# Router logits formed in four column groups of TensorE, and turned back in one step per batch

## The chip, the cores and the metric

The kernel runs on one core of a Trainium2 chip. The metric is the device time of one execution, in microseconds (us). The measured runs give a median over executions; the profile is one further execution, recorded by the hardware profiler.

## What is computed

The input `x` is 8 batches of 512 tokens of 256 values. The reference is two residual blocks:

```python
x = x + attn(cond(x, fside, mask, ...), ...)        # block 1
x = x + ffn(cond2(x, cond_64, ...), ...)            # block 2
```

`cond` is a causal attention with 16 heads of 64 and one shared key and value; `attn` mixes the 16 heads within a token. `cond2` is a mixture of eight experts with two shared ones; its router is the first of the two that the change touches:

```python
logits = (x @ wt.T + repeat(g @ wg.T, s)) / 2       # [4096, 8], x in 256, g in 64 values a batch
scores = softmax(logits); topk_w, topk_idx = top_k(scores, 2)
```

`ffn` is an attention with 16 heads of 16, a layer norm, and a hierarchical mixture of experts with the second router, then a layer norm:

```python
gp = softmax(xt @ w_group + b_group)                # 4 groups
ep = softmax(einsum('td,gde->tge', xt, w_expert) + b_expert)   # 2 experts in each
```

## The kernel before

Everything is float32. The work is cut by batches of 512 tokens (`S`), a batch into four tiles of 128 tokens (`NT`). There are four program parts, each a list of steps in a fixed order. Every engine runs the same list and does its own share of each step, in that order: TensorE (PE) in `tensor_*`, VectorE (DVE) in `vector_*`, ScalarE (ACT) in `scalar_*`, GpSimd (POOL) in `gpsimd_*`, and SyncE (SP), which only starts transfers, in `sync_*`. An engine that waits in a step holds up all of its later steps. `w.wait_ge(at(name, key))` waits for the step that signals `did(name, key)`; waits that are already known to be met are left out. Between parts all engines meet (`meet`, L2640).

**Part one** is `cond` for all batches and `attn` for all but the last.

**Part two** (`order_tail`, then `order_two`) begins with the steps `e_weights` and `x_last`. In `e_weights` SP loads the first router's weights (`wt`, `wg`, `cT`, `before`), then seven batches of the first block's result from memory (`e_x`, 512 KB each), the shared experts' weights and some tables. In `x_last` it loads the last batch's input, four tiles, to which POOL adds a bias (L988). The parts of the last batch's `attn` (`hs`, `hv`: products on POOL and DVE at L829, sums on DVE at L841) are woven with the first router's steps and with the shared experts (`shared`, L1246, L1257). The first router's steps are

- `r_init`, one step behind the first part of the woven list `one`: PE forms `g @ wg.T` for the batches (L1201), ACT halves it into `cs` (L1523), DVE fills `ones` (L1310);
- `r_turn`: PE turns a batch's tiles (L1208), ACT writes them to `e_xT` (L1528);
- `r_score`: PE multiplies with `wt`, 8 weight columns against 512 tokens, in two halves of the contraction (L1215); ACT adds `cs` and writes `e_lgT`, 8 partitions by 512 (L1533);
- `r_back`: four transposes turn 8x128 pieces into 128x8 ones in one bank (L1227);
- `r_lgc`, `r_soft`, `r_rank`, `r_cnt`, `r_oh`, `count`, for lots of 3, 4 and 1 batches: softmax, the two best experts and each token's place in its expert's list (mostly DVE). Then POOL scatters the tokens (L1578), and after `slots` it fetches them by expert.

Batches 0 to 6 pass turn, score and back early in part two; the last one at its end, since it needs the last `attn`.

**Part three** is the attention of `ffn`, with the second router at its end. The attention computes scores in four row groups of the array (L1842, L1863), exponentials on ACT (`m_pt`, L2022), and the products with the values in four column groups (`m_av`, L1877):

```python
for j in range(4):
    i = pe.matmul(m.ap[32 * j:32 * j + 32, :], v.ap[:, kt, 4 * g + j, :], p.ap[:, j, :],
                  start=(kt == 0), stop=(kt == NT - 1), tile_position=(0, 32 * j))
```

In the last slot but one of batch 6 (`h_tables`) SP loads the second router's weights and tables, and DVE fills `h_ones` (L2248). Early in batch 7 (`h_load`, L2140) SP loads six batches back (`h_x`), once every store of them is done. In batch 7 the steps `h_turn` (L2177, L2459), `h_score` (L2184, L2464) and `h_back` (L2196) of batches 0 to 5 stand in the slots between the attention's own steps, one triple to three slots; those of batches 6 and 7 follow behind the attention (`last_rows`, L1681 on). They are like the first router's with 12 logits in place of 8. `h_gate` and `h_count`, for lots of 6, 1 and 1 batches, choose the expert (DVE); then POOL scatters (L2489).

**Part four** fetches the tokens by expert, runs the experts, the last layer norm, and writes the output.

Of the kernel before, what the change touches and what calls it, by code (L numbers as in the profile page):

```python
# [175 lines left out]
def at(name, *key):  # L176
    return (name, *key)
# [32 lines left out]
def cols(t):  # L210
    return t[tuple(slice(None) for _ in t.shape)]
# [847 lines left out]
def setup_two(k, nc, ins):  # L1059
# [6 lines left out]
    k.wt = sb("ew_wt", [P, 2, E8])  # L1066
    k.wg = sb("ew_wg", [DH, E8])
# [42 lines left out]
    k.lgT = Ring([sb(f"e_lgT{i}", [E8, S]) for i in range(2)])  # L1110
    k.cs = sb("e_cs", [E8, NB])
# [11 lines left out]
    k.end2 = at_.pos  # L1123

# [5 lines left out]
def route_ring(k, b):  # L1130

    return k.rR if b < NB - 1 else k.rM


def sync_two(k, sp, w, order):
    did, ins = k.c.did, k.ins

    def load(name, i, dst, src):
        sp.dma_start(dst, src).then_inc(*did("d_" + name, i))

    for step, *key in order:
# [53 lines left out]
def tensor_two(k, pe, w, order):  # L1195
    did, ident = k.c.did, k.ident
    for step, *key in order:
        if step == "r_init":
            m = k.rR.take(("cs",), at("e_csc", 0))
            w.wait_ge(at("d_router", 3), m.room)  # L1200
            pe.matmul(m.ap[0:E8, 0:NB], k.wg[:, :], k.cT[:, :], start=True, stop=True).then_inc(*did("e_cs", 0))  # L1201
# [104 lines left out]
def vector_two(k, dv, w, order):  # L1306
    did = k.c.did
    for step, *key in order:
        if step == "r_init":
            dv.memset(k.ones[:, :], 1.0).then_inc(*did("e_ones", 0))  # L1310
        elif step == "r_lgc":
# [3 lines left out]
            dv.tensor_copy(k.lg[:, n0:n1, :], k.rL.of(g).ap[:, 0:(n1 - n0) * E8].rearrange("p (t e) -> p t e", e=E8)).then_inc(*did("e_lgc", g))  # L1315
# [161 lines left out]
def route(k, dv, w, step, g):  # L1477
# [26 lines left out]
    elif step == "r_cnt":  # L1504
        prior = k.before[:, :, :].unsqueeze(1).broadcast_to([P, GT, E8, E8])
        w.wait_ge(at("r_k", g, 0), at("d_router", 3))
        dv.tensor_tensor(c1, c1, prior, ALU.mult).then_inc(*did("r_c", g, 0))
        w.wait_ge(at("r_c", g, 0), at("r_k", g, 1))
        dv.tensor_tensor(c0, c0, c1, ALU.add).then_inc(*did("r_c", g, 1))
        w.wait_ge(at("r_c", g, 1))  # L1510
        dv.tensor_reduce(gv, c0, AX, ALU.add).then_inc(*did("r_c", g, 2))
    else:
        w.wait_ge(at("r_c", g, 2))
        dv.tensor_scalar(k.oh[:, n0:n1, 0, :], gv, 0.5, None, ALU.is_lt)
        dv.tensor_scalar(k.oh[:, n0:n1, 1, :], gv, 1.0, None, ALU.is_equal).then_inc(*did("r_oh2", g))


def scalar_two(k, ac, w, order):
    did = k.c.did
    for step, *key in order:  # L1520
        if step == "r_init":
            w.wait_ge(at("e_cs", 0))
            ac.activation(k.cs[:, :], k.rR.of(("cs",)).ap[0:E8, 0:NB], ACT.Copy, scale=0.5).then_inc(*did("e_csc", 0))  # L1523
# [5 lines left out]
        elif step == "r_score":  # L1529
# [3 lines left out]
            ac.activation(l.ap[:, :], route_ring(k, b).of(("score", b)).ap[0:E8, :], ACT.Identity, bias=k.cs[:, b:b + 1], scale=0.5).then_inc(*did("e_lgT", b))  # L1533
# [557 lines left out]
def setup_four(k, nc, ins):  # L2093
# [4 lines left out]
    k.hlgT = Ring([e["mx"](f"h_lgT{i}", [12, S]) for i in range(2)])  # L2098
# [12 lines left out]
    k.wgx = e["end"]("hw_gx", [P, 2, 12])  # L2111
    k.bgx = e["end"]("hw_bgx", [12, 1])
# [23 lines left out]
def sync_four(k, sp, w, order):  # L2136
    did, ins = k.c.did, k.ins

    def load(name, i, dst, src):
        sp.dma_start(dst, src).then_inc(*did("d_" + name, i))  # L2140

    for step, *key in order:
        if step == "h_tables":
            load("gx", 0, k.wgx[:, :, 0:4], ins["w_group"].rearrange("(c p) g -> p c g", p=P))
            load("bg", 0, k.bgx[0:4, :], ins["b_group"].rearrange("(n o) -> n o", o=1))
            load("bx", 0, k.bgx[4:12, :], ins["b_expert"].rearrange("(n o) -> n o", o=1))
# [302 lines left out]
def scalar_four(k, ac, w, order):  # L2449
    did, ins = k.c.did, k.ins  # L2450

    for step, *key in order:
# [7 lines left out]
        elif step == "h_score":  # L2460
# [3 lines left out]
            ac.activation(l.ap[:, :], k.hA.of(("score", b)).ap[0:12, :], ACT.Identity, bias=k.bgx[:, 0:1]).then_inc(*did("h_lgT", b))  # L2464
# [271 lines left out]
```

## Time and profile before

| | us |
|---|---|
| median of 3 runs | 2408.55 |
| lowest and highest run | 2406.16, 2410.59 |
| span of the profiled execution | 2401.5 |
| PE busy | 2053.0 (85%) |
| DVE busy | 1528.3 (64%) |
| ACT busy | 1161.6 (48%) |
| POOL busy | 1068.8 (45%) |

For the profiled execution its span is the only time given, from its first instruction to its last; the median of the runs is 7.05 us above it. Part two runs from about 1098 to its last expert; the second router's steps run from 2071 to 2209.

How to read the rows: times are in us from the span's start unless marked ns. PE is a matmul, PEld a weight load of TensorE; SPq is the queue in which SP starts transfers. `out<-in` are the program's names with buffer numbers left out; `128*32 128x512` is a weight tile of 128 rows and 32 columns and a moving tile of 128 partitions and 512 elements. One float32 matmul of the program appears as two instructions, a transpose as one. `[11.66 <-POOL prod L829]` is idle time before an instruction, and what ended it.

### The profile page before, as it was taken

Reading aid. Unit: us, or ns where it says so; the run is one execution under the profiler, and the core shown is the slowest. Engines: PE = TensorE matmul, PEld = TensorE weight load, DVE = VectorE, ACT = ScalarE, POOL = GpSimd, SP = SyncE. Lnnn points to the kernel's source line nnn. Section 1 sums busy time; section 2 is a strip of 40 time slices with the busy share of each in tenths; the row PEclk is TensorE's granted clock in tenths of the full one; section 3 lists DMA queues with packets and bytes.
Section 4 is the critical chain, followed back from the end, with each engine's and each line's share of the span. In section 5 each row is a group of like instructions: output and inputs, shape, how many; then the busy total and the mean of one; then the engine's idle time right before and its main releaser. Section 6 shows DMA issues by size and latency. Waiting matters only on the chain.

```text
span 2401.5 us, 33727 instructions
## 1 busy us (share of the span) xinstructions
PE 2053.0 (85%) x11536; PEld 1111.7 (46%) x11536; DVE 1528.3 (64%) x3276; ACT 1161.6 (48%) x2718; POOL 1068.8 (45%) x840
## 2 busy tenths in 40 slices
PE   2999899999989998985678976889999998873997
PEld 1555555555555555552345863223333332221664
DVE  1345868686776768685964545667667766434776
ACT  0776666666666666662112341345555454541221
POOL 0104747474756658474576532112222201117686
PEclk9999999999999999997889997899999999996998
DMA  7315352434410000005035643111111150203232
GB/s 250 116 36 170 101 194 88 132 108 139 136 34 13 14 7 5 14 5 152 25 112 166 194 155 90 43 35 40 45 53 50 40 193 18 73 10 106 78 92 75
DMA packets 175729, 204.60 MB, mean 85 GB/s; under 512 B 19305, under 2 KB 157417, under 8 KB 175306
## 3 DMA queue, kind: packets, MB, share of 16 engines
q1 hardware_dynamic: 116826, 112.57, 14.8%
q0 software_dynamic: 16752, 45.84, 6.3%
q10 hardware_dynamic: 41984, 44.04, 5.4%
q8 instruction: 95, 1.56, 0.3%
q14 instruction: 72, 0.59, 0.1%
HBM read 83.75 MB, written 114.46 MB: 83 GB/s over the span
## 4 chain that ended last, share of the span: by engine, by line
PE 59%; DVE 14%; POOL 9%; ACT 9%; issue 5%; DMA 2%; ACTq 2%; SPq 1%; POOLq 0%; DVEq 0%
PE ps L1863 11%; POOL prod L829 8%; ACT m_pt L2022 6%; PE ps L561 4%; PE ps L588 4%; PE ps L547 3%; PE ps L572 3%; PE ps L598 3%; DVE sc L841 3%; PE ps L1877 3%; DVE pb L712 3%; PE ps L2224 3%; PE ps L1285 3%; PE ps L2232 2%; PE ps L1821 2%
## 5 line engine op out<-in xcount | busy, mean ns | idle before, releaser
L1954 DVE TENSOR_REDUCE m_mx<-ps 128x2 f32<-128x1024 f32 x256 | 311.6, 1224 | 172.3 <-PE ps L1842 171.6
L712 DVE CUSTOM_DVE_ANT_0 pb<-ps,bias,snl 128x128 f32<-128x128 f32 (+3 forms) x512 | 260.4, 547 | 226.6 <-PE ps L561 223.7
L2022 ACT ACTIVATE m_pt<-ps 128x1024 f32<-128x1024 f32 x256 | 260.5, 1024 | 289.2 <-PE ps L1863 289.2
L829 POOL TENSOR_TENSOR prod<-qs,kvs 128x1024 f32<-128x1024 f32 x120 | 283.7, 2390 | 171.8 <-issue 133.0
L829 POOL TENSOR_TENSOR prod<-sc,kvs 128x1024 f32<-128x1024 f32 x120 | 280.5, 2369 | 101.9 <-ACT sc L947 85.8
L1863 PE MATMUL ps<-m_q,m_k 32*128 32x512 f32 x1024 | 274.2, 647 | 50.8 <-ACT m_pt L2022 39.9
L907 ACT ACTIVATE pb<-pb,mst 128x129 f32<-128x129 f32 (+3 forms) x512 | 283.4, 560 | 16.9 <-DVE mst L712 14.9
L1842 PE MATMUL ps<-m_k,m_q 32*128 32x512 f32 x1024 | 276.3, 660 | 8.9 <-DVE m_mx L1954 8.3
L561 PE MATMUL ps<-kz,qT 64*128 64x128 f32 (+3 forms) x1024 | 185.5, 441 | 0.0
L2041 POOL DMA_INDIRECT m_yg<-ye_scratch,e_pos x64 | 63.1, 986 | 270.4 <-DVE m_x L1942 233.1
L572 PE MATMUL ps<-ident,pb 128*128 128x128 f32 x1280 | 179.8, 279 | 0.5 <-DVE mst L712 0.4
L841 DVE TENSOR_REDUCE sc<-prod 128x64 f32<-128x1024 f32 x128 | 152.3, 1210 | 43.1 <-POOL prod L829 42.8
L922 ACT ACTIVATE ptb<-ps 128x384 f32<-128x384 f32 (+1 forms) x256 | 135.5, 545 | 68.9 <-PE ps L572 68.4
L588 PE MATMUL ps<-ptb,vt 128*64 128x512 f32 (+3 forms) x1024 | 156.9, 449 | 11.6 <-DVE xr L786 11.6
L572 PEld LDWEIGHTS ps<-ident,pb 128*128 128x128 f32 x1280 | 140.9, 141 | 55.9 <-issue 43.5
L841 DVE TENSOR_REDUCE ob<-prod 128x64 f32<-128x1024 f32 x128 | 153.2, 1211 | 9.8 <-POOL prod L829 9.8
L1863 PEld LDWEIGHTS ps<-m_q,m_k 32*128 32x128 f32 x1024 | 73.2, 185 | 174.2 <-ACT m_pt L2022 150.4
L1877 PE MATMUL ps<-m_pt,m_va 128*32 128x512 f32 x1024 | 140.5, 612 | 0.0
L547 PE MATMUL ps<-xnT,w_wq 128*128 128x512 f32 x256 | 122.1, 599 | 13.1 <-DVE oTT L724 13.1
L598 PE MATMUL ps<-w_wo,oTT 128*128 128x256 f32 x512 | 122.3, 382 | 3.0 <-DVE oTT L724 3.0
L2054 POOL TENSOR_TENSOR m_lnrs<-m_lnve,mhalf 128x1 f32<-128x1 f32 x32 | 18.1, 565 | 227.9 <-DVE m_lnve L797 227.9
L588 PEld LDWEIGHTS ps<-ptb,vt 128*64 128x64 f32 x1024 | 70.8, 140 | 94.1 <-issue 83.5
(329 smaller groups left out, 3837.4 us busy)
## 6 DMA issues: line engine op xcount, KB each, us to landing
xh_scratch<-zt SPq DMA_DIRECT2D x43, 768.0 KB, 8.2
xe_scratch<-zt ACTq DMA_DIRECT2D x32, 1024.0 KB, 4.5
ye_scratch<-e_ys SPq DMA_DIRECT2D x36, 256.0 KB, 2.1
hw_w<-in_w SPq DMA_DIRECT2D x16, 512.0 KB, 6.0
xin<-in_x SPq DMA_DIRECT2D x8, 512.0 KB, 3.6
bias<-in_fside ACTq DMA_DIRECT2D x8, 512.0 KB, 10.6
y_scratch<-e_y SPq DMA_DIRECT2D x8, 512.0 KB, 3.2
m_x<-y_scratch SPq DMA_DIRECT2D x8, 512.0 KB, 4.1
```

Source lines behind the costliest of these rows:

```text
L561: pe.matmul(ms[j].ap[:, 0:n], q.ap[DH * j:DH * j + DH, t * P:(t + 1) * P], kz.ap[DH * j:DH * j + DH, 0:n], start=False, stop=True, tile_po ...
L572: i = pe.transpose(m.ap[:, j * P:(j + 1) * P], pb[:, SEG[t] + kt * P:SEG[t] + (kt + 1) * P], ident[:, :])
L588: i = pe.matmul(m.ap[DH * j:DH * j + DH, kt * P:S], v.ap[:, kt, :], turned(pt.ap, kt), start=(kt == 0), stop=(kt == NT - 1), tile_position ...
L712: dv.tensor_tensor_reduce(pb.ap[:, j, SEG[t]:SEG[t] + n], rS.of(("S", b, p, t, j)).ap[:, 0:n], k.bias[:, h, CAUSAL[t]:CAUSAL[t + 1]], -1.0 ...
L829: e.tensor_tensor(out, one, two, ALU.mult).then_inc(*k.c.did(*product_done(step, b, t, u)))
L841: dv.tensor_reduce(heads(dst.ap[:, :])[:, 4 * u:4 * u + 4, :], src, AX, ALU.add).then_inc(*k.c.did(step + "_r", b, t, u))
L907: ac.activation(part, part, ACT.Exp, bias=ms[:, 0, j, t:t + 1], scale=-1.0, accum_out=ms[:, 1, j, t:t + 1]).then_inc(*did("exp", b, p, t, j))
L1842: x = pe.matmul(m.ap[:, i, :], band(q.ap, j)[:, t * P:(t + 1) * P], band(kk.ap, j), start=True, stop=True, tile_position=(32 * j, 0))
L1863: x = pe.matmul(m.ap[:, i, :], band(kk.ap, j)[:, kt * P:(kt + 1) * P], band(q.ap, j), start=True, stop=True, tile_position=(32 * j, 0))
L1877: i = pe.matmul(m.ap[32 * j:32 * j + 32, :], v.ap[:, kt, 4 * g + j, :], p.ap[:, j, :], start=(kt == 0), stop=(kt == NT - 1), tile_position ...
L1954: dv.tensor_reduce(x.ap[:, t, 64 * half:64 * half + 64].rearrange("p (i r) -> p i r", i=2)[:, :, 16], score_ring(k, b).of((b, g, t, half)) ...
L2022: ac.activation(p.ap[:, 2 * half:2 * half + 2, :], k.qE.of((b, g, kt, half)).ap, ACT.Exp).then_inc(*did("m_exp", b, g, kt, half))
```

## The change

Both routers: the weights are padded to 32 columns, and each of a batch's four tiles gets its own column group of the array, so that the logits of tile `t` lie in partitions `32t` and on, over 128 tokens. The eviction is 128x128 in place of 8x512 or 12x512. One transpose (first router), or one matmul with columns picked from the identity (second), turns a whole batch's logits back. The padding is filled with zeros by DVE, and SP waits for that before it loads the weights. The biases are loaded once for each group.

```diff
+BAND = 32
@@ setup_two
-    k.wt = sb("ew_wt", [P, 2, E8])
-    k.wg = sb("ew_wg", [DH, E8])
+    k.wt = sb("ew_wt", [P, 2, BAND])
+    k.wg = sb("ew_wg", [DH, NT, BAND])
-    k.lgT = Ring([sb(f"e_lgT{i}", [E8, S]) for i in range(2)])
-    k.cs = sb("e_cs", [E8, NB])
+    k.lgT = Ring([sb(f"e_lgT{i}", [P, P]) for i in range(2)])
+    k.cs = sb("e_cs", [P, NB])
+def bands(ap, rows):
+    return ap.rearrange("p (t r) -> p t r", r=BAND)[:, :, 0:rows]
@@ sync_two, e_weights
-            load("router", 0, cols(k.wt), ...)
-            load("router", 1, cols(k.wg), ins["moe_wg"])
-            load("router", 2, cols(k.cT), ins["condT"][:, 0:NB])
-            load("router", 3, cols(k.before), ins["c_before"])
+            w.wait_ge(at("e_pad", 0), at("e_pad", 1))
+            load("router", 0, k.wt[:, :, 0:E8], ...)
+            for t in range(NT):
+                load("router", 1 + t, k.wg[:, t, 0:E8], ins["moe_wg"])
+            load("router", NT + 1, cols(k.cT), ins["condT"][:, 0:NB])
+            load("router", NT + 2, cols(k.before), ins["c_before"])
@@ tensor_two
-            pe.matmul(m.ap[0:E8, 0:NB], k.wg[:, :], k.cT[:, :], start=True, stop=True).then_inc(*did("e_cs", 0))
+            pe.matmul(m.ap[:, 0:NB], k.wg[:, :, :].rearrange("p t r -> p (t r)"), k.cT[:, :], start=True, stop=True)...
             for c in range(2):
-                i = pe.matmul(m.ap[0:E8, :], k.wt[:, c, :], k.exT[:, b, c, :], start=(c == 0), stop=(c == 1))
+                for t in range(NT):
+                    i = pe.matmul(band(m.ap, t)[:, 0:P], k.wt[:, c, :], k.exT[:, b, c, t * P:(t + 1) * P],
+                                  start=(c == 0), stop=(c == 1), tile_position=(0, BAND * t))
@@ r_back
-            for t in range(NT):
-                n = b * NT + t - LOT[g][0]
-                i = pe.transpose(m.ap[:, n * E8:(n + 1) * E8], l.ap[:, t * P:(t + 1) * P], ident[0:E8, 0:E8])
-            i.then_inc(*did("e_lgb", b))
+            n = b - LOT[g][0] // NT
+            pe.transpose(m.ap[:, n * P:(n + 1) * P], l.ap[:, :], ident[:, :]).then_inc(*did("e_lgb", b))
@@ vector_two, r_init
+            dv.memset(k.wt[:, :, :], 0.0).then_inc(*did("e_pad", 0))
+            dv.memset(k.wg[:, :, :], 0.0).then_inc(*did("e_pad", 1))
             dv.memset(k.ones[:, :], 1.0).then_inc(*did("e_ones", 0))
@@ scalar_two, r_score
-            ac.activation(l.ap[:, :], route_ring(k, b).of(("score", b)).ap[0:E8, :], ACT.Identity, ...)
+            ac.activation(l.ap[:, :], route_ring(k, b).of(("score", b)).ap[:, 0:P], ACT.Identity, ...)
@@ setup_four
-    k.hlgT = Ring([e["mx"](f"h_lgT{i}", [12, S]) for i in range(2)])
+    k.hlgT = Ring([e["mx"](f"h_lgT{i}", [P, P]) for i in range(2)])
-    k.wgx = e["end"]("hw_gx", [P, 2, 12])
-    k.bgx = e["end"]("hw_bgx", [12, 1])
+    k.wgx = e["end"]("hw_gx", [P, 2, BAND])
+    k.bgx = e["end"]("hw_bgx", [P, 1])
@@ sync_four, h_tables
+            w.wait_ge(at("h_pad", 0), at("h_pad", 1))
             load("gx", 0, k.wgx[:, :, 0:4], ...)
-            load("bg", 0, k.bgx[0:4, :], ins["b_group"]...)
-            load("bx", 0, k.bgx[4:12, :], ins["b_expert"]...)
+            for t in range(NT):
+                load("bg", t, k.bgx[BAND * t:BAND * t + 4, :], ins["b_group"]...)
+                load("bx", t, k.bgx[BAND * t + 4:BAND * t + 12, :], ins["b_expert"]...)
@@ tensor_four
             for c in range(2):
-                i = pe.matmul(m.ap[0:12, :], k.wgx[:, c, :], xt.ap[c][:, :], start=(c == 0), stop=(c == 1))
+                for t in range(NT):
+                    i = pe.matmul(band(m.ap, t)[:, 0:P], k.wgx[:, c, :], xt.ap[c][:, t * P:(t + 1) * P],
+                                  start=(c == 0), stop=(c == 1), tile_position=(0, BAND * t))
@@ h_back
-            for t in range(NT):
-                n = b * NT + t - HLOT[g][0]
-                i = pe.transpose(m.ap[:, n * 12:(n + 1) * 12], l.ap[:, t * P:(t + 1) * P], ident[0:12, 0:12])
-            i.then_inc(*did("h_lgb", b))
+            n = 12 * (b * NT - HLOT[g][0])
+            pe.matmul(m.ap[:, n:n + 12 * NT], l.ap[:, :], bands(ident[:, :], 12), start=True, stop=True)...
@@ vector_four, h_tables
+            dv.memset(k.wgx[:, :, :], 0.0).then_inc(*did("h_pad", 0))
+            dv.memset(k.bgx[:, :], 0.0).then_inc(*did("h_pad", 1))
             dv.memset(k.hones[:, :], 1.0).then_inc(*did("h_ones", 0))
```

DVE's copies of the logits (L1315, L2405) and the waits for the loads follow the new places and counts.

## Rows read from the trace of the kernel before

**Rows 1.** Timeline of SP's queue, from 1098: start, us, line, transfer, count.

```profile
1098.89 0.38 SPq L1139 DMA_DIRECT2D ew_wt<-in_moe_wt  x1
1099.32 0.48 SPq L1139 DMA_DIRECT2D ew_wg<-in_moe_wg  x1
...
1113.41 1.85 SPq L490 DMA_DIRECT2D e_x<-in_x  x4
```

**Rows 2.** Timeline of POOL, same stretch; idle before, and releaser, in brackets.

```profile
1119.88 2.77 POOL L988 TENSOR_TENSOR e_x<-e_x,w_bout 128x256 f32<-128x256 f32 x4 [22.11 <-DMA e_x<-in_x]
```

**Rows 3.** Chain of waits in part two: start, us, engine, output, line.

```profile
1114.83 4.92 DMA e_x<-in_x
...
1144.50 2.57 PE ps L1215 x4
...
1269.39 1.90 PE ps L1215 x4
```

**Rows 4.** Timeline of DVE in part two.

```profile
1110.94 0.17 DVE L1310 MEMSET e_ones<- 128x128 f32 x1
...
1124.97 1.22 DVE L841 TENSOR_REDUCE sc<-prod 128x64 f32<-128x1024 f32 x1 [11.66 <-POOL prod L829]
...
1142.14 0.42 DVE L753 TENSOR_TENSOR qs<-ps,w_bq 128x256 f32<-128x256 f32 x1 [2.52 <-PE ps L635]
...
1150.21 0.25 DVE L1492 TENSOR_REDUCE e_sm<-e_lg 128x12 f32<-128x96 f32 x1 [2.37 <-ACT e_lg L1538]
```

**Rows 5.** Chain of waits at the end of part three, scores of batches 2, 6, 7.

```profile
2108.63 1.82 PE ps L2184 x4
...
2163.85 3.14 PE ps L2184 x4
...
2189.07 3.60 PE ps L2184 x4
```

**Rows 6.** Timeline of POOL at the end of part three.

```profile
2178.89 0.73 POOL L2054 TENSOR_TENSOR m_lnrs<-m_lnve,mhalf 128x1 f32<-128x1 f32 x1 [1.47 <-DVE m_lnve L797]
...
2201.25 0.97 POOL L2489 DMA_INDIRECT xh_scratch<-h_x,h_sposi  x1 [0.30 <-issue]
2204.80 1.05 POOL L2489 DMA_INDIRECT xh_scratch<-h_x,h_sposi  x1 [2.58 <-issue]
```

**Rows 7.** L1877: its first four matmuls; all eight, with loads; durations ns min/median/max.

```profile
2122.90 0.64 PE L1877 MATMUL ps<-m_pt,m_va 128*32 128x512 f32 x4
...
2122.90 0.16 PEld L1877 LDWEIGHTS ps<-m_pt,m_va 128*32 128x32 f32 x8 [0.17 <-issue]
2122.90 1.06 PE L1877 MATMUL ps<-m_pt,m_va 128*32 128x512 f32 x8
...
L1877 PEld LDWEIGHTS ps<-m_pt,m_va x1024: 106/109/156, 1532.8 to 2157.5; 128*32 128x32 f32 x171
```

**Rows 8.** ACT: the line L1533 (ns min/median/max), and L941 among the groups (us, ns).

```profile
L1533 ACT ACTIVATE e_lgT<-ps,e_cs x8: 662/678/679, 1113.1 to 1271.3; 8x512 f32<-8x512 f32 x8
...
L941 ACT ACTIVATE kvs<-ps 128x256 f32<-128x256 f32 x32 | 12.2, 380 | 27.8 <-PE ps L641 27.8
```

**Rows 9.** Timeline of PE, a batch's `r_back`.

```profile
1118.68 0.41 PE L1227 MATMUL ps<-ident,e_lgT 8*128 8x8 f32 x4 [0.77 <-ACT e_lgT L1533]
```

**Rows 10.** Timelines of SP, DVE and PE around `h_tables` and `h_load`.

```profile
2071.84 0.44 SPq L2140 DMA_DIRECT2D hw_gx<-in_w_group  x1
...
2072.87 0.17 DVE L2248 MEMSET h_ones<- 128x128 f32 x1
...
2080.92 4.67 SPq L2140 DMA_DIRECT2D h_x<-x_scratch  x6
...
2085.31 0.66 PE L2177 MATMUL ps<-ident,h_x 128*128 128x128 f32 x4 [0.43 <-DMA h_x<-x_scratch]
...
2087.40 0.66 PE L2177 MATMUL ps<-ident,h_x 128*128 128x128 f32 x4 [1.43 <-ACT h_xT L2459]
```

**Rows 11.** One stretch: length, busy by engine (instructions), granted clock, DMA share, GB/s.

```profile
2104.50:2113.00 8.50, 7.92 (x41) 2.73 (x42) 0.00 (x0) 3.64 (x7) 0.00 (x0) 0.80 0.00 0
```

More of the change, by code:

```diff
@@ L1142, in sync_two @@
         if step == "e_weights":
-            load("router", 0, cols(k.wt), ins["moe_wt"].rearrange("(c p) e -> p c e", p=P))
-            load("router", 1, cols(k.wg), ins["moe_wg"])
-            load("router", 2, cols(k.cT), ins["condT"][:, 0:NB])
-            load("router", 3, cols(k.before), ins["c_before"])
+            w.wait_ge(at("e_pad", 0), at("e_pad", 1))
+            load("router", 0, k.wt[:, :, 0:E8], ins["moe_wt"].rearrange("(c p) e -> p c e", p=P))
+            for t in range(NT):
+                load("router", 1 + t, k.wg[:, t, 0:E8], ins["moe_wg"])
+            load("router", NT + 1, cols(k.cT), ins["condT"][:, 0:NB])
+            load("router", NT + 2, cols(k.before), ins["c_before"])
             for b in range(NB - 1):
@@ L1199, in tensor_two @@
             m = k.rR.take(("cs",), at("e_csc", 0))
-            w.wait_ge(at("d_router", 3), m.room)
-            pe.matmul(m.ap[0:E8, 0:NB], k.wg[:, :], k.cT[:, :], start=True, stop=True).then_inc(*did("e_cs", 0))
+            w.wait_ge(at("d_router", NT + 2), m.room)
+            pe.matmul(m.ap[:, 0:NB], k.wg[:, :, :].rearrange("p t r -> p (t r)"), k.cT[:, :], start=True, stop=True).then_inc(*did("e_cs", 0))
         elif step == "r_turn":
@@ L1314, in vector_two @@
             n0, n1 = LOT[g]
-            dv.tensor_copy(k.lg[:, n0:n1, :], k.rL.of(g).ap[:, 0:(n1 - n0) * E8].rearrange("p (t e) -> p t e", e=E8)).then_inc(*did("e_lgc", g))
+            dv.tensor_copy(k.lg[:, n0:n1, :], bands(k.rL.of(g).ap[:, 0:(n1 - n0) * BAND], E8)).then_inc(*did("e_lgc", g))
         elif step in ("r_soft", "r_rank", "r_cnt", "r_oh"):
@@ L1505, in route @@
         prior = k.before[:, :, :].unsqueeze(1).broadcast_to([P, GT, E8, E8])
-        w.wait_ge(at("r_k", g, 0), at("d_router", 3))
+        w.wait_ge(at("r_k", g, 0), at("d_router", NT + 2))
         dv.tensor_tensor(c1, c1, prior, ALU.mult).then_inc(*did("r_c", g, 0))
@@ L1522, in scalar_two @@
             w.wait_ge(at("e_cs", 0))
-            ac.activation(k.cs[:, :], k.rR.of(("cs",)).ap[0:E8, 0:NB], ACT.Copy, scale=0.5).then_inc(*did("e_csc", 0))
+            ac.activation(k.cs[:, :], k.rR.of(("cs",)).ap[:, 0:NB], ACT.Copy, scale=0.5).then_inc(*did("e_csc", 0))
         elif step == "r_turn":
@@ L1532, in scalar_two @@
             w.wait_ge(at("e_lg", b), at("e_csc", 0), l.room)
-            ac.activation(l.ap[:, :], route_ring(k, b).of(("score", b)).ap[0:E8, :], ACT.Identity, bias=k.cs[:, b:b + 1], scale=0.5).then_inc(*did("e_lgT", b))
+            ac.activation(l.ap[:, :], route_ring(k, b).of(("score", b)).ap[:, 0:P], ACT.Identity, bias=k.cs[:, b:b + 1], scale=0.5).then_inc(*did("e_lgT", b))
         elif step == "r_soft":
@@ L2143, in sync_four @@
         if step == "h_tables":
+            w.wait_ge(at("h_pad", 0), at("h_pad", 1))
             load("gx", 0, k.wgx[:, :, 0:4], ins["w_group"].rearrange("(c p) g -> p c g", p=P))
-            load("bg", 0, k.bgx[0:4, :], ins["b_group"].rearrange("(n o) -> n o", o=1))
-            load("bx", 0, k.bgx[4:12, :], ins["b_expert"].rearrange("(n o) -> n o", o=1))
+            for t in range(NT):
+                load("bg", t, k.bgx[BAND * t:BAND * t + 4, :], ins["b_group"].rearrange("(n o) -> n o", o=1))
+                load("bx", t, k.bgx[BAND * t + 4:BAND * t + 12, :], ins["b_expert"].rearrange("(n o) -> n o", o=1))
             for g in range(4):
@@ L2193, in tensor_four @@
             w.wait_ge(at("h_lgT", b))
-            for t in range(NT):
-                n = b * NT + t - HLOT[g][0]
-                i = pe.transpose(m.ap[:, n * 12:(n + 1) * 12], l.ap[:, t * P:(t + 1) * P], ident[0:12, 0:12])
-            i.then_inc(*did("h_lgb", b))
+            n = 12 * (b * NT - HLOT[g][0])
+            pe.matmul(m.ap[:, n:n + 12 * NT], l.ap[:, :], bands(ident[:, :], 12), start=True, stop=True).then_inc(*did("h_lgb", b))
         elif step == "h_count":
@@ L2463, in scalar_four @@
             w.wait_ge(at("h_lg", b), at("m_mT", NB - 1, G4 - 1), l.room)
-            ac.activation(l.ap[:, :], k.hA.of(("score", b)).ap[0:12, :], ACT.Identity, bias=k.bgx[:, 0:1]).then_inc(*did("h_lgT", b))
+            ac.activation(l.ap[:, :], k.hA.of(("score", b)).ap[:, 0:P], ACT.Identity, bias=k.bgx[:, 0:1]).then_inc(*did("h_lgT", b))
         elif step == "h_gate":
```

4 lines of the change are left out of this document (2 added, 2 removed).

## The prediction

> **What bounds the kernel now.** I read the profile's page, the chain of waits, the queue of the sync engine (SP), and then each step that the change touches, in order of time. TensorE (PE) is busy for 85% of the span, but the change is decided where engines wait, so I work by place and not by share.
>
> *First place, the start of the second program part.* SP issues `e_weights` and behind it the four loads of `x_last` [rows 1]. GpSimd (POOL) waits 22.11 us for those loads before its `e_x` [rows 2]. The chain of waits runs through just this: SP's issues, the DMA `e_x<-in_x`, `e_x`, `prod`, VectorE's (DVE) `sc` [rows 3]; DVE stands idle 11.66 us in front of that `sc` [rows 4]. So a microsecond that SP loses ahead of `x_last` is lost by all.
>
> *Second place, the end of the third part.* In the last attention batch PE and ScalarE (ACT) take turns, and the second router's scores stand on the chain [rows 5]. Behind it the logits of batches 6 and 7 are links of a serial chain, with POOL's scatters beside it [rows 5, 6].
>
> **A score.** Before, 4 matmuls of 512 columns take 1.90 us at full clock [rows 3]: 4 rounds of 0.43 and a tail of 0.17. After there are 16 of 128 columns. Do column groups overlap? The attention's `L1877` has that form, 32 weight columns at four positions: its eight 512-column matmuls take 1.06 us, the first four together 0.64, their eight weight loads 0.16 [rows 7]; in single file eight would take 3.6. So I take 4 rounds of 0.107 (a quarter of 0.43) and the tail, 0.6 us, and allow 0.1 for 32 instructions where there were 8: 0.7 us, gain 1.2. At half clock 3.60 [rows 5] becomes 4 x 0.213 + 0.2 = 1.05. Bounds: 0.6 us, and the old 1.90 if nothing overlaps.
>
> **The eviction.** ACT's 8x512 takes 0.68 us [rows 8]. No row shows 128x128 from such a source; 128x256 takes 0.38 [rows 8] and is an upper bound but for the bias. I take 0.35, gain 0.33 (bounds 0.2 and 0.4).
>
> **The turn back.** Four small transposes take 0.41 us [rows 9]; one full transpose I take as 0.27, gain 0.13 (a loss is excluded: it is one of the four with more columns). In the second router it becomes a matmul, two weight loads and two short passes for four of each: I take no gain, and up to 0.2 lost where it can no longer run beside `L1863`, whose rows of the array it now uses too.
>
> **Term 1, SP's new wait.** `e_weights` now waits for `e_pad`, which DVE writes in `r_init`. DVE comes there at 1110.94, where it fills `e_ones` now, in 0.17 [rows 4]; two more such fills, overlapping, end at 1111.2. SP begins at 1111.3 in place of 1098.89 [rows 1]: 12.4 us. Then `ew_wg` is loaded four times, three more at 0.48 and a gap [rows 1]: 1.5. Queued behind: the seven `e_x` loads, the shared experts' weights, the tables, `x_last`, and then the experts' weights, which nobody needs before they are in. The whole train moves: **+13.9 us** (low end 12.4, the extra loads free). PE's `r_init` waits too, some 8 us, and its first turn for `e_x`, but the scores of batches 0 to 2, about 3.5 us each then, are through before ACT's late `sc`, behind which they are held now as well.
>
> **Term 2, inside the first router.** The chain passes `e_lgT`, `L1227`, `L635`, then `L1215` at half clock, 2.57 us [rows 3], and `e_lgT` again; DVE idles 2.52 and 2.37 us for it [rows 4]. Of the first idle 0.6 goes (eviction and turn), of the second 1.9 (a score 1.5 shorter, an eviction 0.33), of which PE may give back 0.8 by being at half clock for the next turns. **-2.1** (ends -1.5, -2.5). The other batches' scores lie beside DVE's work: nothing.
>
> **Term 3, its last batch.** Turn, score [rows 3], eviction, back, copy in a row with nothing beside them: 1.2 + 0.33 + 0.13, **-1.65**.
>
> **Term 4, SP in the third part.** `h_tables` waits for two more fills on DVE, where `h_ones` is filled at 2072.87: SP starts at 2073.15 in place of 2071.84, 1.3 us [rows 10]. Six more tiny loads, each somewhat under the 0.44 of the first one [rows 10], 2.3 us. `h_load` is the next step but one on this queue, with no gap, and PE's first `h_turn` already waits for its first landing [rows 10]: 3.6 us later. Its second turn waits 1.43 us for ACT, until 2087.40 [rows 10]; of that I estimate 0.75 as ACT still finishing `m_pt`, which will be over by then. **+2.85** (end 3.6; no delay at all is excluded by the DMA as the releaser in that row).
>
> **Term 5, batches 0 to 5 of the second router.** In even ones `L2184` [rows 5] stands before `L1863`, for which ACT waits: 1.6 (partly half clock) + 1.2 + 1.2. In odd ones the eviction is queued behind two `m_pt` of ACT, and once the score is short ACT is what is late: I take 0.75, 0.25 and 1.0. Together 6.0, less 0.5 for PE being longer at half clock after Term 4's stall: **-5.5** (ends -3.5, -7.5).
>
> **Term 6, batches 6 and 7.** Scores of 3.14 and 3.60 at half clock [rows 5] lose 2.0 and 2.6, an eviction 0.33: 4.9 us on DVE's chain. But POOL's scatters run back to back until 2202.2, with little but one wait of 1.47 us in them [rows 6]. They would end at about 2200.5, and the last batch's would start 0.3 behind them, at 2200.8 in place of 2204.80 [rows 6]: **-4.0** (end -3.3).
>
> **Sum:** 13.9 - 2.1 - 1.65 + 2.85 - 5.5 - 4.0 = **+3.5 us**. The profiled span of 2401.5 becomes 2405.0; what lies between it and the median, 7.05, I leave: 2408.55 becomes **2412.0 us**. A measurement of this kernel can tell about 0.2% (4.8 us) from no change, so this is the upper half of no change. With the low ends, and with the high ends, the case reaches from 2407 to 2416.5.
>
> **Rivals.**
> - *The weight loads are not hidden.* Each round then pays a load of 0.109 [rows 7] and 0.107 of columns: 4 x 0.216 + 0.17 = 1.03 us, 0.33 more than forecast at full and some 0.65 at half clock, 3.2 over the scores that count: +6.7, 2415.2 us, slower. Against: the loads of `L1877`'s second round lie within its first [rows 7]. For: that round lasts 0.43, a new one 0.107, no longer than a load. 10%. The Trainium skill (TensorE: Matmul & The Clock Gate, Part 3) states that a weight load overlaps matmuls in flight only if it goes to another row group, which these never do. By that rule this rival is the case; `L1877`'s eight loads in 0.16 us speak against the rule.
> - *The column groups don't overlap at 128 columns.* 16 x 0.107 + 0.17 = 1.88: the score gains nothing, Terms 2, 3, 5 and 6 shrink to -0.9, -0.5, -0.5, -0.5: +14.4, 2423 us, slower. It decides from a score of some 1.4 us on. Against: rows 7. 7%.
> - *PE's clock.* PE has less to do in the last attention batch, and the granted clock is down to 0.80 in one stretch there already [rows 11]. If two more stretches of 9 us fell from full to that, 1.8 us each: +7.1, 2415.7 us, slower. 8%.
> - *The wait doesn't count.* If `x_last` were covered, Term 1 is gone: -10.4, 2398 us, faster. Against: 22.11 us of idle time in front of it [rows 2]. For: DVE has idle stretches behind it, where some could be caught up. 9%.
>
> **How the numbers follow.** 66% for the forecast's case: 46 within 0.2%, 17 above, 3 below. With the rivals: slower 17 + 10 + 7 + 8 = 42%, same 46%, faster 3 + 9 = 12%. The range, 2404 to 2421, leaves out the last rival and the second, and a few hundredths at the case's own edges.
>
> **What would show it.** SP's `ew_wt` at about 1111.3; POOL's `e_x` at 1133.8; a score of 16 matmuls in 0.7 us, an eviction of 0.35; `h_tables` issued behind DVE's fills, and PE waiting some 3 us more for the first `h_x`; the last batch's scatters 0.3 us behind the others. The prediction is wrong if POOL's `e_x` isn't some 13 us late, if a stage behind it takes that up, or if a score takes over 1 us.

## The result, and the profile of the kernel after

The changed kernel takes 2410.15 us (median of 12 runs, 2406.49 to 2416.83), the kernel before, on the same chip, 2404.43 us (12 runs, 2398.50 to 2410.59). The ratio is 1.0028, with a 95% interval of 1.0015 to 1.0041: slower by 6.7 us (3.6 to 9.9; the medians alone differ by 5.7), a little more than the 0.2% that can be told from no change. The profiled execution spans 2405.5 us where that of before spanned 2401.5, so the profiles can explain only 4.0 us of the difference. The twelve executions of the kernel after have mean granted clocks of TensorE between 0.946 and 0.952; the profile of before has 0.955.

First SP's queue and its followers in part two, from the timeline of the kernel after (start, duration, engine, instruction, idle time before it and what ended it), which answer to [rows 1, 2, 4]:

```profile
1109.07 0.11 DVE L1318 MEMSET ew_wt<- 128x64 f32 x1
1109.39 0.38 SPq L1145 DMA_DIRECT2D ew_wt<-in_moe_wt  x1
...
1114.93 0.59 PE L1209 MATMUL ps<-ew_cT,ew_wg 64*128 64x8 f32 x2 [7.57 <-DMA ew_before<-in_c_before]
...
1124.91 1.86 SPq L491 DMA_DIRECT2D e_x<-in_x  x4
1130.43 2.76 POOL L989 TENSOR_TENSOR e_x<-e_x,w_bout 128x256 f32<-128x256 f32 x4 [34.73 <-DMA e_x<-in_x]
1135.51 1.22 DVE L842 TENSOR_REDUCE sc<-prod 128x64 f32<-128x1024 f32 x1 [23.86 <-POOL prod L830]
```

SP starts right behind DVE's fills. POOL's `e_x` begins 10.55 us later than before and DVE idles 23.86 us in front of `sc`, where it idled 11.66 us before. This execution's first part had run 1.87 us ahead of the other's (DVE's fill is at 1109.07, not at 1110.94), though nothing in the first part was changed; so the delay that the change makes here is 10.55 + 1.87 = 12.4 us.

The last batch of the first router, in the chain of waits after (start, duration, what), answers to the last scores of [rows 3]:

```profile
1277.58 0.69 PE ps L1224 x16
1278.27 0.02 issue
1278.30 0.38 ACT e_lgT L1543
1278.67 0.14 issue
1278.81 0.31 PE ps L1236
1279.12 0.02 issue
1279.14 0.20 DVE e_lg L1325
```

A score of 0.69 us in place of 1.90, an eviction of 0.38 in place of 0.69, a turn of 0.31 in place of 0.40. Then the shared expert (`L1254` after, `L1246` before), in windows of PE (length, PE busy, granted clock, DMA share, GB/s), after and then before:

```profile
1295.00:1300.00 5.00, 5.00 (x10) 0.71 0.26 105
```

```profile
1291.00:1296.00 5.00, 5.00 (x16) 1.00 0.15 52
```

The third part, SP and PE in the timeline of after, against [rows 10]:

```profile
2081.55 0.38 SPq L2150 DMA_DIRECT2D hw_gx<-in_w_group  x1
...
2091.93 4.28 SPq L2150 DMA_DIRECT2D h_x<-x_scratch  x6
...
2096.30 0.82 PE L2189 MATMUL ps<-ident,h_x 128*128 128x128 f32 x4 [2.80 <-DMA h_x<-x_scratch]
2097.89 1.11 PE L2189 MATMUL ps<-ident,h_x 128*128 128x128 f32 x4 [0.77 <-ACT h_xT L2473]
2100.64 1.08 PE L2197 MATMUL ps<-h_xT,hw_gx 128*32 128x128 f32 x16
```

And its end, POOL's scatters and the conversion of their indices on DVE, against [rows 6]:

```profile
2201.66 0.17 DVE L2354 CAST h_sposi<-h_spos 128x4 int32<-128x4 f32 x1
...
2204.04 1.17 POOL L2503 DMA_INDIRECT xh_scratch<-h_x,h_sposi  x1 [0.30 <-issue]
2207.76 0.96 POOL L2503 DMA_INDIRECT xh_scratch<-h_x,h_sposi  x1 [2.54 <-issue]
```

POOL is free at 2205.2 and the indices are there since 2201.8, yet the last batch's first scatter starts at 2207.76. It was 2204.80 before, where the indices came at 2202.5, just behind POOL's coming free at 2202.2:

```profile
2202.31 0.17 DVE L2340 CAST h_sposi<-h_spos 128x4 int32<-128x4 f32 x1
```

The fourth part begins 3.1 us later than before (2220.66 less 2217.55), but its first transposes of `h_hb` are 4.2 later. PE's timeline after, then before:

```profile
2220.66 1.08 PE L2227 MATMUL ps<-ident,h_xs 128*128 128x128 f32 x4 [21.19 <-DMA h_xs<-xh_scratch,h_gix]
2221.93 3.78 PE L2236 MATMUL ps<-hw_w,h_sT 128*128 x4 [0.19 <-ACT h_sT L2489]
...
2227.86 0.60 PE L2252 MATMUL ps<-ident,h_hb 128*128 128x128 f32 x4
```

```profile
2217.55 1.09 PE L2215 MATMUL ps<-ident,h_xs 128*128 128x128 f32 x4 [17.50 <-DMA h_xs<-xh_scratch,h_gix]
2218.83 3.08 PE L2224 MATMUL ps<-hw_w,h_sT 128*128 x4 [0.19 <-ACT h_sT L2475]
...
2223.69 0.60 PE L2240 MATMUL ps<-ident,h_hb 128*128 128x128 f32 x4
```

The same instructions take longer after PE's idle time: their five us from 2221.8 on run at a granted clock of 0.54, the corresponding five of before, from 2218.7 on, at 0.76.

### The profile page after: what moved, and what is told of

It reads as the page before. It is cut to its first block, busy times and chain, and to the rows that moved or that the text cites. A ratio compares the mean times of both kernels' runs of the same rounds, so it can differ in the third digit from the quotient of the medians.

```text
span 2405.5 us, 34045 instructions
## 1 busy us (share of the span) xinstructions
PE 2039.3 (85%) x11688; PEld 1118.0 (46%) x11688; DVE 1528.2 (64%) x3280; ACT 1156.3 (48%) x2718; POOL 1068.5 (44%) x840
## 4 chain that ended last, share of the span: by engine, by line
PE 57%; DVE 13%; POOL 10%; ACT 9%; issue 5%; DMA 2%; ACTq 2%; SPq 1%; POOLq 0%; DVEq 0%
PE ps L1873 11%; POOL prod L830 8%; ACT m_pt L2032 6%; PE ps L589 4%; PE ps L562 4%; PE ps L548 3%; PE ps L573 3%; PE ps L599 3%; DVE sc L842 3%; DVE pb L713 3%; PE ps L1887 3%; PE ps L1293 3%; PE ps L1831 2%; PE ps L2236 2%; PE ps L2244 2%
```

## The experiments

Each ratio is to the kernel before on the same chip in the same session. That matters for the first four, which ran on a chip where the kernel before took 2443 us; on the others it took 2401 to 2403. "Under the kernel after" means under its ratio of 1.0028, which was measured in another session; such differences are uncertain by some 4 to 6 us.

**1. The wait alone, in the kernel before.**

```diff
+            dv.memset(k.wt[:, :, :], 0.0).then_inc(*did("e_pad", 0))
+            dv.memset(k.wg[:, :], 0.0).then_inc(*did("e_pad", 1))
             dv.memset(k.ones[:, :], 1.0).then_inc(*did("e_ones", 0))
...
+            w.wait_ge(at("e_pad", 0), at("e_pad", 1))
             load("router", 0, cols(k.wt), ins["moe_wt"]...)
```

> The kernel before, whose DVE fills ew_wt and ew_wg (in their old small shapes) in r_init, and whose SP waits for these fills ahead of e_weights; nothing else of the change. Term 1 alone (the wait is on the path, with nothing behind it to take it up): ew_wt issued at about 1109 to 1111 in place of 1098.9, POOL's e_x later by the same 10.5 to 12.4 us, and the whole 10 to 12.4 us slower (ratio about 1.0045). The wait doesn't count (rival): POOL's e_x is as late, but the time is within 2 us of before. The wait costs because of the loads' number and not of the wait: no delay at all at POOL's e_x.

Ratio 1.0049 (1.0033 to 1.0066), 12 us slower. From its timeline:

```profile
1108.79 0.38 SPq L1139 DMA_DIRECT2D ew_wt<-in_moe_wt  x1
1128.95 2.78 POOL L988 TENSOR_TENSOR e_x<-e_x,w_bout 128x256 f32<-128x256 f32 x4 [33.25 <-DMA e_x<-in_x]
```

One wait for two fills of 0.07 us costs more than the whole change does. Some of the 12 us may be clock, since these executions also have the lower mean granted clock (0.943 to 0.953, the kernel before 0.946 to 0.955). The rival that the wait doesn't count falls.

**2. The change with its two fills earlier.** DVE has 7.6 us of idle time at the head of part two; the fills move there, SP's wait stays.

```diff
-        if step == "r_init":
+        if step == "e_weights":
             dv.memset(k.wt[:, :, :], 0.0).then_inc(*did("e_pad", 0))
             dv.memset(k.wg[:, :, :], 0.0).then_inc(*did("e_pad", 1))
+        elif step == "r_init":
             dv.memset(k.ones[:, :], 1.0).then_inc(*did("e_ones", 0))
```

> The kernel after, with DVE's two fills moved from r_init to the head of its part two, where its idle time of 7.6 us lies; SP's wait stays. Term 1 is the wait: SP issues ew_wt at about 1099, POOL's e_x comes 10 to 12 us earlier than in after, and the time is 10 to 12 us under after, about 5 under before (ratio to before about 0.998). If the three more loads of ew_wg were what costs, or if the wait didn't count: within 2 us of after (ratio to before 1.002 to 1.003).

0.9980 (0.9965 to 0.9995): 4.9 us faster than before, so some 11.7 under the kernel after (1.0028 less 0.9980, of 2443). From its timeline:

```profile
1096.75 0.11 DVE L1318 MEMSET ew_wt<- 128x64 f32 x1 [0.18 <-DVEq L2655]
1097.09 0.38 SPq L1145 DMA_DIRECT2D ew_wt<-in_moe_wt  x1
...
1119.27 2.76 POOL L989 TENSOR_TENSOR e_x<-e_x,w_bout 128x256 f32<-128x256 f32 x4 [23.74 <-DMA e_x<-in_x]
```

The three more loads of `ew_wg` are still there, and they are not free: `e_x` follows `ew_wt` by 22.18 us here and by 21.04 in the kernel after, where run 1, without them, has 20.16. That is 1 to 2 us, small against the wait.

**3 and 4. `x_last` ahead of `e_weights` on SP's queue,** once in the kernel after, once in the kernel before.

```diff
-    out = [("e_weights",), ("x_last",)] + [x for part in start for x in part]
+    out = [("x_last",), ("e_weights",)] + [x for part in start for x in part]
```

> The kernel after, with SP's x_last ahead of e_weights and its wait. Reading of term 1 by x_last alone (PE's own lateness behind the router's weights costs nothing): POOL's e_x no longer waits, DVE's 23.9 us of idle time in front of sc shrink to a few, 12 us or more under after. Rival, term 1 has two roads: the router's weights and the e_x loads come late as well, PE's r_init and its first turn (now 7.6 and 1.8 us idle) hold the first part's last batch in PE's queue, and only a part comes back, 0 to 8 us under after.

> The kernel before with SP's x_last ahead of e_weights, nothing of the change. If the x_last load is what the stage waits for, DVE's 11.7 us of idle time in front of sc go but for what the late router weights (1.8 us later) give back: 7 to 11 us under before (ratio 0.9955 to 0.997). If it is covered by something else that is nearly as late: within 3 us of before.

In the kernel after: 0.9942 (0.9920 to 0.9964), 21 us under it. In the kernel before: 0.9954 (0.9936 to 0.9972), 11 us under it. POOL and PE in the timeline of the first, then POOL in that of the second:

```profile
1100.94 2.77 POOL L989 TENSOR_TENSOR e_x<-e_x,w_bout 128x256 f32<-128x256 f32 x4 [5.63 <-DMA e_x<-in_x]
1115.93 0.59 PE L1209 MATMUL ps<-ew_cT,ew_wg 64*128 64x8 f32 x2 [8.84 <-DMA ew_before<-in_c_before]
```

```profile
1099.67 2.77 POOL L988 TENSOR_TENSOR e_x<-e_x,w_bout 128x256 f32<-128x256 f32 x4 [5.80 <-DMA e_x<-in_x]
```

DVE has no idle time left in front of `sc` in either. The 11 us of before are the 11.66 of [rows 4]; the kernel after gets these and a good part of the wait. But not all of it: PE still idles 8.84 us for the router's weights. What that costs shows in the time from PE's start in part two (`L622`, 1096.89 in the kernel after, 1098.96 before) to POOL's first scatter (1181.09, 1172.16): 73.2 us before, 84.2 after, 73.2 in run 2, 61.5 in run 4, 66.4 in run 3, and 60.5 in run 12 below, which has run 2's fills as well (60.7 in run 7, which has them too). So with `x_last` first the wait still costs 5.9 us (66.4 less 60.5) by way of PE. Both theories of the expectation were half right: the second road, by way of PE, is real, but it was the shorter one, and the gain was far above the 8 us that this theory allowed.

**5. The four matmuls of a column group in a row.** In both scores.

```diff
-            for c in range(2):
-                for t in range(NT):
+            for t in range(NT):
+                for c in range(2):
                     i = pe.matmul(band(m.ap, t)[:, 0:P], ...)
```

> The kernel after; in both scores the loop over the four column groups is outside and that over the two halves of the sum inside, so that four matmuls in a row go to one group and only the ends of the groups can run side by side: 13 rounds in place of 4. If the short score comes of the groups running side by side, the 16 matmuls take 13 x 0.107 + 0.17 = 1.6 us at full clock (0.65 in after), 2.9 at half, and the time rises by 7 to 12 us over after (ratio to before about 1.006). If it comes of the 128 columns alone or of cheaper instructions, the score stays at 0.65 and the time is that of after (1.003).

1.0029 (1.0016 to 1.0042), the kernel after over again. PE and ACT in its timeline:

```profile
1278.00 0.67 PE L1224 MATMUL ps<-e_xT,ew_wt 128*32 128x128 f32 x16 [0.79 <-ACT e_xT L1538]
1278.76 0.37 ACT L1543 ACTIVATE e_lgT<-ps,e_cs 128x128 f32<-128x128 f32 x1 [0.81 <-PE ps L1224]
```

ACT starts 0.76 us after the score does, 0.72 in the kernel after (1278.30 less 1277.58), so it isn't a matter of how ends are recorded. My expectation of 1.6 us failed. Either the groups had nothing to do with it, or PE doesn't need them in turn.

**10. Groups apart (made to decide that).** Unused matmuls in PE's idle time in `r_init`.

```diff
+            for i in range(8):
+                pe.matmul(band(m.ap, i % NT)[:, 0:P], ident[:, 0:BAND], ident[:, :], start=True, stop=True, tile_position=(0, BAND * (i % NT)))
+            for i in range(8):
+                pe.matmul(band(m.ap, 0)[:, 0:P], ident[:, 0:BAND], ident[:, :], start=True, stop=True, tile_position=(0, 0))
+            for i in range(8):
+                pe.matmul(m.ap[0:E8, 0:P], ident[:, 0:E8], ident[:, :], start=True, stop=True)
+            for i in range(2):
+                pe.matmul(m.ap[0:E8, :], ident[:, 0:E8], ident[:, :].unsqueeze(1).broadcast_to([P, NT, P]), start=True, stop=True)
```

> The kernel after with 26 more matmuls (52 instructions) on PE in r_init, where it is idle for 7.6 us; their output is not used. Eight of 128 columns in turn over the four column groups; eight of 128 columns all in the first group; eight of 128 columns with 8 weight columns and no group named; two of 512 columns with 8 weight columns. At full clock 128 columns have been worth 0.107 an instruction. If groups run side by side: 16 instructions take 16 x 0.107 / 4 = 0.43 in turn over the groups and 1.7 all in one group. If each narrow matmul is simply quick: 0.43 to 0.6 for both. The form without a group: 1.7 if columns count, 0.43 to 0.6 if narrow weights alone make it quick. The last: 1.7 (4 x 0.43). Time as after's.

PE's timeline, matmuls and then weight loads (PEld):

```profile
1109.48 0.64 PE L1210 MATMUL ps<-ident 128*32 128x128 f32 x16
1109.95 1.91 PE L1212 MATMUL ps<-ident 128*32 128x128 f32 x16
1111.69 1.91 PE L1214 MATMUL ps<-ident 128*8 128x128 f32 x16
1113.44 1.88 PE L1216 MATMUL ps<-ident 128*8 128x512 f32 x4
...
1109.48 0.38 PEld L1210 LDWEIGHTS ps<-ident 128*32 128x32 f32 x16 [0.76 <-issue]
1109.84 1.75 PEld L1212 LDWEIGHTS ps<-ident 128*32 128x32 f32 x16
```

The one execution took 2410.2 us. From start to start: 0.47 us in turn over four groups, 1.74 all in one, 1.75 without a group. The factor is 3.7. The groups do run side by side, and narrow weights alone bring nothing. Together with run 5: four groups are needed, but not in turn. How far ahead in its queue PE takes a matmul for a free group was not measured.

**6. `h_tables` ten steps earlier.**

```diff
-        out[30].append(("h_tables",))
+        out[20].append(("h_tables",))
```

> The kernel after, with the step h_tables (the second router's fills and 22 loads) ten steps earlier in part three, on all engines. If term 4 is what SP's queue costs (measured +1.9 us at PE's second turn), SP's h_x loads come earlier, PE's 2.8 us of idle time in front of its first h_turn go, and the time is 1.5 to 3 us under after (ratio to before 1.0015 to 1.002), with an earlier point only if the table loads were on the path before the change too. If h_x's own waits bind, h_x is no earlier and nothing changes.

1.0054 (1.0036 to 1.0071): slower than the kernel after by 6 us. PE's wait for the first `h_x` is gone, but a worse one has come. Its chain of waits, then POOL in its timeline:

```profile
2072.88 0.44 SPq L2150
2073.32 0.04 issue
2073.37 2.16 DMA m_z<-y_scratch
```

```profile
2075.59 0.72 POOL L2059 TENSOR_TENSOR m_z<-m_z,mw_bo 128x256 f32<-128x256 f32 x1 [11.31 <-DMA m_z<-y_scratch]
```

Ten us of table loads now stand in front of `m_z`, which DVE and then PE (idle 4.94 us) need. I had looked at who stands behind the tables at step 30 and not at step 20.

**7. All three moves** (2, 3 and 6 together).

> The kernel after with all three moves: DVE's fills of ew_wt and ew_wg at the head of part two, SP's x_last ahead of e_weights, h_tables ten steps earlier. The x_last move alone gave 0.9942 of before, with PE still idle 8.8 and 1.8 us behind the late router weights. If those waits were on the path: another 4 to 9 us there and 2 from the tables, 0.990 to 0.992. If DVE is the bound there once x_last is early: 2 to 3 us in all, 0.993.

0.9927 (0.9915 to 0.9940): 17.5 us faster than before, with run 6's loss in it. That is the figure I gave for DVE as the bound, but run 6's loss, which I hadn't counted, is in it, and the stretch to the first scatter shortened from 66.4 to 60.7 us; so the late router weights had been on the path, and the ratio alone doesn't decide.

**8. Marks on POOL** ahead of the late scatter.

```diff
+            if n == HLOT[HLAST][0]:
+                po.memset(k.hnil[:, 0:4], 0.0)
+                w.wait_ge(at("h_gs", n // NT))
+                po.memset(k.hnil[:, 4:8], 0.0)
+                w.wait_ge(at("h_id", n // NT))
+                po.memset(k.hnil[:, 8:12], 0.0)
             w.wait_ge(at("h_gs", n // NT), at("h_id", n // NT), at("hc_pos", hlot(n // NT)))
+            if n == HLOT[HLAST][0]:
+                po.memset(k.hnil[:, 12:16], 0.0)
```

> The kernel after with four memsets of 128x4 on POOL as marks ahead of the last batch's first h_scatter: before its waits, after the wait for h_gs, after that for h_id, after that for hc_pos. In after POOL was free at 2205.2, all three were fulfilled by 2201.8, and the scatter started at 2207.8. If a late signal holds POOL, the 2.5 us lie between the marks. If the gap is POOL's own (its next code or its descriptors), they lie before the first mark or behind the last one, and the marks themselves cost about 0.1 us each; if it is a cost of waiting at all, each mark has a share. Time within 2 us of after.

1.0035 (1.0016 to 1.0053). POOL's timeline, the first and the last mark and the scatter:

```profile
2206.03 0.12 POOL L2504 MEMSET h_nil<- 128x4 f32 x1
...
2206.14 0.12 POOL L2511 MEMSET h_nil<- 128x4 f32 x1
2208.39 0.96 POOL L2512 DMA_INDIRECT xh_scratch<-h_x,h_sposi  x1 [2.13 <-issue]
```

All waits are passed by 2206.14; the 2.13 us lie behind the last mark, in the DMA itself. No signal is late. A count shows more: in each of the twelve profiles with this kernel's 4096 bytes for descriptors, the scatters stop behind their 28th, in part two (2.27 us at 1239.75 before) as in part three. (In the four profiles of the slower chip the stop in part three is 6.2 to 8.3 us, which the next expectation overlooks.)

**9. A larger store for POOL's descriptors.** Two small tiles of the first part lie elsewhere to make room.

```diff
-    nc = bacc.Bacc("TRN2", target_bir_lowering=False, num_devices=1, dynamic_dma_scratch_size=4096)
+    nc = bacc.Bacc("TRN2", target_bir_lowering=False, num_devices=1, dynamic_dma_scratch_size=4608)
```

> The kernel after with 4608 bytes in place of 4096 for the descriptors of POOL's DMAs (two small tiles of the first part lie elsewhere for that). In every trace so far a run of scatters stands still for 2.1 to 2.6 us behind its 28th, wherever its data are (29th and 57th of part two, 29th of part three). Theory: the store of descriptors is full after 28 and POOL waits until the last is through; with an eighth more that comes after 32. Then the 29th scatter of part two follows in 0.3 us and the 33rd does not, the 29th scatter of part three follows in 0.3 us, the last four lie about 2.2 us earlier, and the time is 2 to 4.5 us under after (ratio to before about 1.0015). Rival, it is POOL's code that has to be fetched or something else of the place: the gaps stay behind the 28th, time that of after.

1.0026 (1.0011 to 1.0041), no gain. But the stop has moved, by three scatters and not by four. The 31st and the 32nd scatter of part three in its timeline, and the first fetch behind them:

```profile
2210.55 0.96 POOL L2503 DMA_INDIRECT xh_scratch<-h_x,h_sposi  x1 [0.30 <-issue]
2213.90 0.96 POOL L2503 DMA_INDIRECT xh_scratch<-h_x,h_sposi  x1 [2.39 <-issue]
2217.42 0.97 POOL L2511 DMA_INDIRECT h_xs<-xh_scratch,h_gix  x1 [2.56 <-SPq L2654]
```

Part two's stops moved alike, from the 29th and 57th DMA to the 32nd and 63rd: a period of 28 became one of 31 with an eighth more room. So the store's size sets it. There are 32 scatters, so the stop still fell inside them and was still paid. One more place would have put it behind them; no memory was left for that, and it wasn't tried.

**11. The third part's queue shortened.** Fills ten steps earlier, the six more loads behind the first `h_x`, tables in place.

```diff
-        if step == "h_tables":
+        if step == "h_fill":
             dv.memset(k.wgx[:, :, :], 0.0).then_inc(*did("h_pad", 0))
             dv.memset(k.bgx[:, :], 0.0).then_inc(*did("h_pad", 1))
+        elif step == "h_tables":
             dv.memset(k.hones[:, :], 1.0).then_inc(*did("h_ones", 0))
...
+        out[20].append(("h_fill",))
         out[30].append(("h_tables",))
```

> The kernel after; DVE's fills of hw_gx and hw_bgx come ten steps earlier, so that SP's wait ends at once, and the six more loads of hw_bgx stand behind the first load of h_x in place of ahead of it; the tables stay where they are. Term 4 (a later queue of SP makes PE's first h_turn late, +1.9 measured): SP's first load of h_x is issued 3 us earlier, PE's 2.8 us of idle time there go to about 0.4, and the time is 1 to 2.5 us under after (ratio to before about 1.002). If PE loses it again in batch 0 behind ACT: within 1 us of after.

1.0023 (1.0012 to 1.0034). The 0.0005 under the kernel after is 1.2 us and less than the intervals; the profiles show it more sharply: PE's first `h_turn` has no wait,

```profile
2092.29 0.66 PE L2193 MATMUL ps<-ident,h_x 128*128 128x128 f32 x4
2094.87 0.66 PE L2193 MATMUL ps<-ident,h_x 128*128 128x128 f32 x4 [1.93 <-ACT h_xT L2478]
```

and the last batch's first scatter is at 2204.72 where it was 2207.76, of which 0.8 us were there in part two already. So the wait is shown to be SP's queue, but a gain in the time isn't shown.

**12. The best of all:** 2, 3, 9 and 11 together.

> The kernel after with all that the runs so far favour: DVE's fills of the first router at the head of part two, x_last first on SP's queue, the second router's fills early and its six loads behind the first h_x, and 4608 bytes for POOL's descriptors. The first two with the tables moved (which cost 5 alone) gave 0.9927; without that loss 3 to 5 us less, with tables short and the ring another 3 to 5: 0.9895 to 0.991 of before, about 22 to 25 us faster.

2380.05 us, 0.9910 (0.9895 to 0.9926): 21.6 us faster than before, at the weak end of what I expected and not to be told from run 7. It is what this change is worth in the right order, with the 11 us of run 4 that don't need it: by an estimate across two chips, some 10 us are the change's own.

## Why the prediction was right, and where it wasn't

The forecast was 2412.0 us, 3.5 above the median known then; measured were 2410.15 and a difference of 6.7 (3.6 to 9.9). The time lies in the range, the difference in the case "slower" (42%), not in "same" (46%). The absolute time fits better than the difference does, and by luck: the twelve runs of before came out 4.1 us under the first three. The ends listed with the terms add up to 2408.1 and 2416.1, not to the prediction's 2407 and 2416.5; nothing hangs on it.

Point by point, from the two profiles:

- **Term 1, +13.9: measured +12.4.** The wait is exact; its price is shown by runs 1 and 2. Of the 1.5 for three more loads of `ew_wg` these two profiles show nothing, by accident: SP did spend 1.9, but `ew_cT` took 0.6 us in place of 1.52, as it did in runs 1 and 4 without those loads, and the `x_last` load landed 0.95 sooner after its issue (5.52, not 6.47). Against run 1 the loads cost 0.9.
- **Term 2, -2.1: -1.8**; another 0.6 up to the last batch. **Term 3, -1.65: -1.60.** The sizes of the score (0.7 forecast, 0.65 to 0.69 measured), of the eviction (0.35, 0.38) and of the turn (0.27, 0.31) held.
- **Not foreseen, +1.7.** Behind the slots, PE is idle for 3.3 us in both kernels and then runs the shared expert. Before it did so at a granted clock of 1.00, after at 0.71 in the five us shown above: `L1254`'s sixteen take 8.8 us where they took 7.1. The fall is no oddity of this execution: eleven of the fourteen profiles show one in these instructions, with runs 1 and 4 among them, which have nothing of the new scores (granted clocks of 0.77 and 0.78 there); only those of before and of runs 2 and 3 don't. So it is rather the profile of before that is the rarer case, and that the change brings the fall is not shown. It is the third rival's mechanism (8%) at a place I hadn't named.
- **Term 4, +2.85: +1.9.** PE waits 2.80 for `h_x`, as forecast some 3 us; the six loads took 2.0 but the tables behind them were issued quicker than before (3.67 in place of 4.87 for the eight of `hw_gx`). Run 11 shows the term to be SP's queue.
- **Term 5, -5.5: -6.1** in all, but not as split. From one batch's second turn to the next one's, batches 0 to 5 gave 0.3, 0.6, 2.7, 0, 1.4 and 1.1 us. Batch 0 should have given 1.6: PE was at a clock of 0.72 behind its wait, where before it was at 0.81, and that ate most of the shorter score. Of batch 2's 2.7 half is clock.
- **Term 6, -4.0: -1.4. The step that failed.** It was "the last batch's would start 0.3 behind them". I took the 2.58 us in front of that scatter [rows 6] for the wait for its indices, which came at just that time. Runs 8 and 9 show another cause: POOL stands still for over 2 us behind the 28th scatter, whatever DVE has ready, and a larger store of descriptors moves the stop. So only about the 1.47 of idle time among the scatters went, and the stop of 2.54 stayed.

With the 1.9 us by which this execution was ahead, these make 12.4 - 1.9 - 1.8 - 0.6 - 1.6 + 1.7 + 1.9 - 6.1 - 1.4 = +2.6 of the profiles' +4.0. Of the other 1.4, 1.1 are the start of part four, where PE ran at the lower clock for longer, as shown above; 0.3 lie in the third part ahead of `h_x` and have no cause that I can name. From PE's first turn in part four to its transposes of `h_hb` it takes 6.14 us in the profile of before, 7.20 after, and 6.28 to 7.66 in the other twelve, in no order that the change explains; so here too the profile of before is the favourable one. Term 1 was 1.5 too dear, Term 4 1.0 too dear and Term 6 2.6 too generous, and that these nearly cancelled was luck.

One thing none of the terms holds. The mean granted clock of the kernel after is 0.946 to 0.953 in the result and in runs 5, 9 and 11; the kernel before has 0.953 to 0.962 in the sessions of those runs, and runs 7 and 12, which start the router's fills early and `x_last` first, have 0.954 to 0.960. So some of the measured 6.7 us is probably clock over the whole kernel; how much, and what lowers it, is not shown.

**The rivals.** *The weight loads are not hidden*: no. Sixteen loads take 0.38 us and lie inside the score's 0.65. In run 10 even sixteen loads of 0.11 to one and the same group add nothing: 1.74 us are 16 x 0.109, the columns alone. The Trainium skill (TensorE: Matmul & The Clock Gate, Part 3) says that a weight load overlaps matmuls in flight only if it goes to another row group; all of these use all rows, so the trace doesn't agree. The same section of the Trainium skill says that matmuls start and end strictly in their order. By that, run 5's score would have taken about 1.6 us (an estimate: 13 rounds of 0.107 and a tail of 0.17), and it took 0.67; here too the measurement decides. *The groups don't overlap*: no, by the 3.7 of run 10. *The wait doesn't count*: no, by run 1. *PE's clock*: in part, 1.7 and 1.1 us in these two profiles and a lower mean over all executions, as told; how much of it belongs to the change is open.

## What to carry to other kernels

A wait on a DMA queue is priced by the most urgent load behind it, not by the load that it guards: here two fills of 0.1 us, placed at the wrong point of DVE's program, cost 12 us and hid all that the change gained. Before you add one, ask which idle stretch of the filling engine lies earlier, and whether the urgent load can go first; and before you move a block of loads, look at who stands behind it in its new place. Idle time that coincides with the arrival of data is not thereby caused by it: look for the same gap at another place in the trace, at a fixed count, before you book its removal.

## What the runs showed of the hardware that I had not expected

- POOL's indirect DMAs of 128 rows issue every 1.26 us, but behind 28 scatters comes a stop with 4096 bytes for descriptors, and behind 31 with 4608. It takes 2.1 to 2.7 us; in part three of the four runs on the slower chip it took 6.2 to 8.3. In part two the first 28 have pauses of up to 9.5 us among them and the stop comes all the same; the fetches and scatters of part four, 117 in the profile of before, show no such stop. What empties the store is not shown.
- Matmuls on four column groups run side by side also if each group's stand in a row in the queue: 0.67 us in place of 0.65.
- A stall of 2.8 us of PE, in front of the second router, was followed by a stretch at a granted clock of 0.72 (2092.5 to 2102), where before it was 0.81 (2085 to 2094); it took back most of what a score shorter by 1.65 us (1.08 for 2.73) gave.
